# A cross-attention and mixture-of-experts layer: TensorE's order within one pipeline step

## The reference

```python
x = x + xattn(layernorm(x), ctx, ctx, mask)      # 16 heads of 16, 77 keys, softmax
n = layernorm(x)
h = n + layernorm(n, g1, b1) @ attn_w.T
t = layernorm(h, g2, b2)
top2 of t @ gate_w.T -> weights of 2 of 8 experts
out = h + sum over the 2 experts of  w_e * (silu(t @ gate_e.T) * (t @ up_e.T)) @ down_e.T
x = x + out
```

## Time and profile before

| | |
|---|---|
| median of 3 runs | 650.5 us (649.15 to 650.72) |
| the profiled execution's own time | 648.87 us |
| its span | 647.1 us |
| mean granted clock of PE | 0.887 of full speed |
| busy, share of the span | PE 82%, DVE 58%, POOL 52%, ACT 39% |
| tile stage | from about 26.5 us to about 235 us of the span |

### The profile page before, as it was taken

The page is one execution under the profiler, slowest core; times in us unless marked ns, Lnnn a source line. Parts: engine busy times, 40 slices in busy tenths (PEclk is TensorE's granted clock), DMA queues, the critical chain, the costliest instruction groups (busy, mean ns, idle before and its releaser), DMA issues.

```text
span 647.1 us, 13759 instructions
## 1 busy us (share of the span) xinstructions
PE 529.1 (82%) x3325; PEld 460.0 (71%) x3326; DVE 377.4 (58%) x882; ACT 251.1 (39%) x492; POOL 334.7 (52%) x422
## 2 busy tenths in 40 slices
PE   3389898888797515899999299999999999999770
PEld 2278777777686314788888188878878888788660
DVE  1558989888986573744344656474474434836430
ACT  1257556555454242433223252342343333425120
POOL 5356665675675465653343527456355533654320
PEclk9879778877878556999999699999999999999895
DMA  7850100000000105171121064507206311030113
GB/s 213 280 220 18 34 17 17 33 16 16 22 28 18 33 17 180 55 239 27 25 33 24 21 190 122 138 14 200 62 5 202 69 25 24 8 49 8 16 18 140
DMA packets 27089, 46.58 MB, mean 72 GB/s; under 512 B 9718, under 2 KB 22544, under 8 KB 26768
## 3 DMA queue, kind: packets, MB, share of 16 engines
q1 hardware_dynamic: 15312, 35.77, 16.4%
q0 software_dynamic: 9088, 9.52, 8.9%
q10 hardware_dynamic: 2656, 0.91, 0.7%
HBM read 36.67 MB, written 11.61 MB: 75 GB/s over the span
## 4 chain that ended last, share of the span: by engine, by line
PE 55%; DVE 17%; issue 12%; DMA 4%; POOL 4%; DVEq 4%; ACT 1%; POOLq 0%; SPq 0%; ACTq 0%
PE psum L1159 13%; PE psum L1160 12%; PE psum L1161 12%; PE psum L1189 4%; PE psum L1044 4%; DVE split_w L953 3%; DVEq L366 3%; PE psum L1039 3%; DVE tb_hi L999 3%; PE psum L1097 2%; PE psum L1060 2%; POOL rstd L502 2%; DMA wk<-in_wkT 1%; PE psum L1198 1%; DVE stats L720 1%
## 5 line engine op out<-in xcount | busy, mean ns | idle before, releaser
L1159 PE MATMUL psum<-split_w,tb_hi 128*128 x288 | 119.7, 416 | 27.0 <-DVE split_w L953 16.7
L1160 PE MATMUL psum<-split_w,tb_hi 128*128 x288 | 115.0, 399 | 0.0
L1161 PE MATMUL psum<-split_w,tb_lo 128*128 x288 | 114.9, 399 | 0.0
L1159 PE MATMUL psum<-split_w,aT_hi 128*128 x288 | 84.4, 293 | 1.3 <-DVE aT_lo L989 1.2
L1159 PEld LDWEIGHTS psum<-split_w,tb_hi 128*128 128x128 f32 x288 | 55.7, 193 | 39.5 <-issue 29.4
L1160 PE MATMUL psum<-split_w,aT_hi 128*128 x288 | 81.5, 283 | 0.0
L1161 PE MATMUL psum<-split_w,aT_lo 128*128 x288 | 81.4, 283 | 0.0
L381 POOL TENSOR_TENSOR split_w<-w_raw,split_w (+1 forms) x8 | 46.5, 5811 | 60.8 <-DVE split_w L959 50.9
L590 POOL DMA_INDIRECT acc_rows<-o_sb,add_at x36 | 60.2, 1673 | 33.8 <-POOL add_at L588 33.8
L989 DVE TENSOR_TENSOR aT_lo<-psum,aT_hi 128x512 fp32r<-128x512 f32 x72 | 46.3, 685 | 51.2 <-ACT aT_hi L695 51.2
L975 DVE TENSOR_SCALAR o_sb<-psum,blk 128x256 f32<-128x256 f32 x36 | 17.4, 484 | 94.1 <-issue 82.5
(11 more groups left out here) (155 smaller groups left out, 1064.8 us busy)
## 6 DMA issues: line engine op xcount, KB each, us to landing
w_raw<-in_experts SPq DMA_DIRECT2D x24, 768.0 KB, 4.5
w_raw<-in_experts SPq DMA_DIRECT2D x2, 3072.0 KB, 13.2
x_sb<-in_x SPq DMA_DIRECT2D x8, 256.0 KB, 5.0
z_rows<-rows SPq DMA_DIRECT2D x16, 128.0 KB, 1.7
acc_rows<-x_sb SPq DMA_DIRECT2D x16, 128.0 KB, 1.7
ceil_f<-in_mask ACTq DMA_DIRECT2D x2, 308.0 KB, 11.5
blk<-lists POOLq DMA_DIRECT2D x36, 1.0 KB
rows<-z_rows,gather_at POOLq DMA_INDIRECT x36, 3.9
```

The costliest lines, as they stand in the source:

```text
L1159: nc.tensor.matmul(dst, hi, w_hi, start=first, stop=False)
L1160: nc.tensor.matmul(dst, hi, w_lo, start=False, stop=False)
L1161: return nc.tensor.matmul(dst, lo, w_hi, start=False, stop=last)
```

## The change

The scores' loop becomes a function `scores(m)`. Its first half stays where the loop stood, its second half goes behind the q products, and `s_ps` is raised there. The aw product goes from between the second and third round of transposes into P times V, behind the first 5 of its 11 chunks (the split of the wait for `pT_done` moves from chunk 8 to chunk 5). No instruction is added or taken away, and no other engine's order changes.

```diff
+                def scores(m):
+
+                    n, par = number(t2), t2[1]
+                    pe.wait_ge(q_done, KD * n + m + 1)
+                    for r in range(ROW_GROUPS):
+                        last = nc.tensor.matmul(bank[r][:, m * PAIR * KEYS:(m + 1) * PAIR * KEYS],
...
-                    for m in range(KD):
-                        pe.wait_ge(q_done, KD * n + m + 1)
-                        for r in range(ROW_GROUPS):
...
-                    last.then_inc(s_ps, 1)
+                    scores(0)
                 if within(t4, TILES):
...
                     last.then_inc(q_ps, 1)
+                if within(t2, TILES):
+                    scores(1).then_inc(s_ps, 1)
...
                 if within(t3, TILES):
                     weights_T(1).then_inc(pT_ps, 1)
-                if within(t5, TILES):
-                    pe.wait_ge(uT_done, KD * (number(t5) + 1))
-                    row_product(h_bank, uT[:, t5[1], :, :], aw_sb).then_inc(aw_ps, 1)
-                if within(t3, TILES):
                     weights_T(2).then_inc(pT_ps, 1)
...
                     pe.wait_ge(pT_done, PT_ROUNDS * n + 2)
-                    weighted_values(0, 2 * 4)
-                    pe.wait_ge(pT_done, PT_ROUNDS * (n + 1))
-                    weighted_values(2 * 4, CHUNKS).then_inc(o_ps, 1)
+                    weighted_values(0, 5)
+                if within(t5, TILES):
+                    pe.wait_ge(uT_done, KD * (number(t5) + 1))
+                    row_product(h_bank, uT[:, t5[1], :, :], aw_sb).then_inc(aw_ps, 1)
+                if within(t3, TILES):
+                    pe.wait_ge(pT_done, PT_ROUNDS * (number(t3) + 1))
+                    weighted_values(5, CHUNKS).then_inc(o_ps, 1)
```

More of the change, by code:

```diff
@@ L1063, in weighted_values @@
                     return done
+                def scores(m):
[3 more added lines that the diff above has]
+                        last = nc.tensor.matmul(bank[r][:, m * PAIR * KEYS:(m + 1) * PAIR * KEYS],
+                                                qT[r * STRIP:(r + 1) * STRIP, par, m, :],
+                                                k_pair[r * STRIP:(r + 1) * STRIP, par, m, :, :].rearrange("p q k -> p (q k)"),
+                                                start=True, stop=True)
+                    return last
                 if within(t1, TILES):
```

## The result

The changed kernel took 705.26 us (median of 4 runs, 702.75 to 708.17) beside 649.83 us (648.54 to 650.72) for the kernel before: a ratio of 1.0856, 95% interval 1.0808 to 1.0905, so 55 us slower. The profiled execution has a span of 706.4 us against 647.1, a granted clock of 0.84 against 0.887.

What follows compares the result with a forecast made beforehand. The prediction took a loop of waits between DVE and POOL to bound the tile stage. 25.8 + 9.1 + 5.2 + 2.5 = 42.6 us on the profiled 648.87 made 691.5, given as 691, range 670 to 707.

Steps and rivals of the forecast that it cites:

- the loop: Tile stage: DVE's first third of a step, POOL's roots, lists and subtraction, `picked`, the search, again DVE; 12.19 us.
- both places: The late aw product delays `h`, 25.8 us; the scores' late second half delays the maxima, 9.1 + 5.2 + 2.5 us.
- the cover of 4.72 us: POOL's roots and list transfers start the subtraction 4.72 us after `mv` anyway, hiding first maxima ready by then.
- the sum: All delays added: 25.8 + 9.1 + 5.2 + 2.5 = 42.6 us.
- The mixed-clock case: PE at half clock 40% of the time, as reckoned: 691 us, own range 680 to 700, chance 0.60.
- the half-clock rival: PE at half clock throughout, since longer idling brings the low clock: 58.6 us slower, 707 us, chance 0.14.
- 7.7 us for the scores: Early steps without list transfers to cover late scores: 2.5 us in step 3, 5.2 us in steps 4 to 7.
- 2.5 + 1.3 us: Step 3: attention-weight transposes wait for DVE's reading of scores, 2.5 us; step 4: POOL waits for the maximum, 1.3 us.
- The rival "faster": Better filled PE waits give full clock and PE's work sets the step: 646 us, chance 0.04.
- "hidden": POOL's list transfers, not `mv`, set the subtraction, so late `h` costs nothing: only 7.7 us remain, 657 us, chance 0.05.

Runs made afterwards that it cites:

- the move of the transfers: Kernel before, with POOL's two list transfers put behind its subtraction instead of ahead of it: 636.93 us, ratio 0.9812.
- The filled kernel: Changed kernel plus 16 unread identity transposes per step, 6 ahead of PE's wait for the attention output, 10 ahead of that for the top-2 search: 685.77 us.
- the aw product alone: Kernel before with only the aw product moved into P times V, split as in the change, scores as before: 677.31 us, ratio 1.0410.
- the scores alone: Kernel before with only the scores split as in the change, aw product and P times V as before: 674.66 us, ratio 1.0369.
- the filled kernel before: Kernel before plus 16 unread identity transposes in each step, ahead of PE's same two waits: 652.80 us, ratio 1.0030.

## Why the prediction was right, and where it was off

The direction, the loop and both places held. Each was shown by taking it away: the aw product ahead of the wait costs nothing, the scores ahead of the q products 5.5 us instead of 23.9, and the loop of DVE and POOL was shortened directly by the move of the transfers, with the amount that the cover of 4.72 us less 3.41 for the maximum allows. As forecast, 14 `h` wait that had not waited so before; they wait 28.7 us in sum, beside 25.8. But the change cost 55.4 us where the sum had 42.6. The mixed-clock case was to end at 700, and the half-clock rival, 707, came closer, though its condition did not hold. The range held 705 only because it took in a part of that rival; so far it was luck. Two terms were too small.

*The clock.* "Taking the clock of 40% half" was read from the kernel before. After the change the granted clock in the nine steps is 0.69, about 62% at half, and all nine q products are at 1.8 to 1.9 us instead of seven. POOL then waits 1.9 us a step for the maxima (19.3 in 10; 1.75 in the step shown), where I had 1.3 for half clock: half of the scores by itself takes 0.90 us, not 0.7. The aw product made `h` wait 2.1 us (21.1 in 10) instead of 1.84. The step became 3.57 us longer, against 25.7 / 9 = 2.9; that is less than the two waits together, since DVE's search now ends sooner behind the subtraction (the last section). The filled kernel shows that this is the clock and not PE's place alone: at full clock the same order costs 1.29, and `h` waits 1.3 us.

Why the clock fell is shown only in part. The change moved work from in front of PE's waits to behind them, and PE idled longer in front; before P times V 1.8 us in the mean (16.0 in 9) against 1.2 (9.5 in 8). Filling the two waits brought the clock to 1.00. The Trainium skill ("TensorE: Matmul & The Clock Gate", "What's actually happening") has the low clock as the default, which activity releases, and the filling agrees with that. But the longer wait before P times V does not by itself bring the fall: with the aw product alone PE idled there 21.0 us in 11 times, 1.9 in the mean, and the clock stayed at 0.80. With the scores alone it was 0.78, and yet eight of the nine q products ran at half clock.

One price was too small without the clock. The first five chunks hold 10 of the 20 products of P times V, a half rather than 5/11, and took 1.31 us at full clock and 2.17 at half, beside the 1.10 and 1.72 that I had. And the ranks did not have the slack that I gave them: DVE waited for them 7.3 us in 8 steps before. That decided nothing: in the filled kernel before this wait fell to 4.3 us, and no time was won.

*The start.* Up to step 8 the sum had 7.7 us for the scores and two waits of `h`, 11.4; it measured 20.6, of which the scores alone make 12.2 and the aw product alone 5.4 (step 8 at 78.00); 3 us only both together cost. Steps 3 and 4 were put at 2.5 + 1.3 us. The x1 of step 5 came 8.2 us later (53.27 against 45.06); up to 1.8 us of that is the start's own scatter, since it came at 45.22 to 46.82 in the three kernels that move only the aw product, which has no part in these steps. PE after, in step 3:

```profile
38.63 2.37 PE L1051 MATMUL psum<-ident,p_sb 128*128 128x128 f32 x10 [1.72 <-DVE s_sb L744]
41.35 4.45 PE L1060 MATMUL psum<-v_chunks,pT 128*128 128x34 f32 x20 [0.35 <-ACT pT L623]
```

The transposes start 3.25 us later than in the earlier trace rows, as the chain that I added up would have it and a little more; but PE had to idle for that, and P times V then ran at half clock, 4.45 us instead of 2.52, where I had carried nothing further. The fill does not change this: in the filled kernel the same P times V takes 4.45 us too, and step 8 begins 18.8 us later than before. The steps behind it, 5 to 7, were 1.2 to 1.3 us longer in the run of the scores alone, as forecast.

The drain (three waits of `h` at 1.84, 5.5 us) measured 6.6 with the expert stage, which thus lost nothing worth naming. The rival "faster" falls with the fill in the kernel before, "hidden" with the aw product alone. What the two parts cost together beyond their sum, 5 us, I put down to the clock, 0.69 in the steady part against 0.78 and 0.80 with one part. That is argued, not tried; the waits fit it: `h` waits 2.1 us against 1.9 (20.6 in 11) with the aw product alone, POOL 1.9 us for the maxima against 1.8 (18.3 in 10) with the scores alone.

## What to carry to other kernels

Before a product is moved to fill another engine's wait, ask who reads it and when: behind a wait for the search it had joined the loop, though PE idled on both sides of it. An engine that is not on the loop may be served late only by the slack at that place, and here that slack was another engine's own work (the list transfers, 1.3 us), which is itself better moved. And do not price the moved work by the clock of the old order: here the order itself moved the share at half clock from 40% to 62%.

## What was not expected of the hardware

In both kernels one short DVE operation of the step shown lasted long while POOL subtracted, but not the same one. Before, `picked` lasted until the second part of the subtraction had ended (3.02 us). After, it starts within the first part of the subtraction. The copy behind it before, and then DVE's timeline after:

```profile
133.66 0.17 DVE L841 COPY pair<-tokens 128x2 int32 x1
```

```profile
135.99 0.52 DVE L831 TENSOR_TENSOR picked<-hot,place 128x16 f32<-128x16 f32 x1
...
136.68 1.00 DVE L841 COPY pair<-tokens 128x2 int32 x1
```

`picked` ends about half way through POOL's 2.39 us from 135.26, and the integer copy lasts 1.00 us and ends with the second part. The search ends 0.68 us after the subtraction instead of 1.04, so this step gets 0.36 us of POOL's wait back. That POOL held them is argued from the common ends. In the kernel before, `picked` had started 0.58 us ahead of the subtraction, during a list transfer of POOL, and still ended behind it.
